# Row slots of the expert routing worked out tile by tile between later score maxima, and fewer zero products on TensorE

## The chip, the cores and the metric

The kernel runs on one core of a Trainium2 chip. The metric is the device time of one execution in microseconds (us). The engines are TensorE (PE, with its weight loads as PEld), VectorE (DVE), ScalarE (ACT), GpSimd (POOL) and SyncE (SP), which here only issues DMAs. Each runs its own list of instructions in order and waits on semaphores for the others.

## The reference

For x of 1024 tokens by 256 columns, xn is x normalised per row, and the result is x + attention(xn) + experts(xn).

```python
q, k, v = xn @ wq.T, xn @ wk.T, xn @ wv.T          # 16 heads of 16, q and k rotated (RoPE)
scores = where(causal, -inf, q @ k.T / sqrt(16))
att = softmax(scores) @ v @ wo.T
logits = xn @ gate_weight.T                         # 64 experts, 8 for each token
topk_w, topk_idx = top_k(softmax(logits), 8); topk_w /= sum(topk_w)
# each token's row goes to its 8 experts, rows of one expert stand together
out = (silu(rows @ w_gate[e]) * (rows @ w_up[e])) @ w_down[e]
y = sum(out of the token's 8 rows * topk_w)
```

## The kernel before, in words

The front part normalises x, projects it, rotates q and k, splits them in a high and a low part and stores these parts in DRAM (`qk_parts`). The 16 heads are worked in 4 groups of 4 (`g` from 0 to 3). For each group SP loads the parts back in the layout that the scores want (`stage(g, c)`, once for each half `c` of the 1024 tokens), into `qz` and `kz`. `stage(0, 1)`, the second half of group 0, is issued when the last store of `qk_parts` has landed.

The softmax needs the largest score of each query ahead of the scores themselves. So each group has two passes. The first pass is made of 38 "max" units: PE computes a block of up to 512 score columns into one of three PSUM banks (`max_scores`, L1001 and the mask L1005), and DVE reduces it (`use_max`, L1449). A bank is free when DVE has reduced the unit three places ahead. When the first half's maxima are there (`neg`, c = 0, behind the third block of query tile 7), PE transposes them (L1019), DVE negates them into `neg_hi` and `neg_lo` (L1462, L1463), and SP writes them as two more rows of `qz` (`place_negmax`, L495). The second pass then computes the scores (`scores`, L1030, L1033), ACT takes the exponentials (L825), and PE multiplies them with v (`pv`, L1047). Its 12 steps go through key tiles; steps 0 to 3 belong to the first half of the queries, steps 4 to 11 to the second half, and step 4 waits for the second `neg`.

The order in which max units stand between score steps is written out by `attention_order` from the table `MAXIMA_AT`, whose entries say how many 128-column blocks are to be done by which step. `g = -1` is the stretch ahead of the first score. In it and in steps 0 to 3 of group 0 (`FILL_UNTIL = CT`, CT is 4) each max unit is followed by one product of zeros into an unused bank (`keep_busy`, L1011).

The experts' routing lies beside this. PE counts the choices (`counts`, banks 3 and 4), DVE makes from the counts the first row of each expert and a map of row numbers (`count_and_map`, L1336 to L1339), and for each of the 8 token tiles three small instructions: eight row numbers per token, the same beside the token's row, and the same as integers (L1343, L1344, L1346). In the kernel before all of that stands on DVE ahead of the first maximum. POOL waits for each tile's numbers and sends the tile's rows to DRAM with 8 indirect DMAs (L733, 64 in all). SP waits for all 64 and loads the experts' rows (`load_rows`, L525, L527). The experts run between group 1 and group 2 and begin on PE with L1088.

Of the kernel before, what the change touches and what calls it, by code (L numbers as in the profile page):

```python
# [10 lines left out]
ALU = mybir.AluOpType  # L11
# [6 lines left out]
NT = N // P  # L18
# [8 lines left out]
K = 8  # L27
# [8 lines left out]
ID, SLOT_AT = D, D + K  # L36
# [5 lines left out]
SLOT_BASE = float(1 << 14)  # L42
# [7 lines left out]
B_BANKS, PV_BANK, A_BANKS = (0, 1, 2), 3, (5, 6, 7)  # L50
RING, GU_BANKS, EXTRA_BANK = (0, 1, 2), (5, 3), 7
HALF = N // 2
CT = NT // 2
SLOTS = 3
STEPS = [(0, kt) for kt in reversed(range(CT))] + [(1, kt) for kt in reversed(range(NT))]
NS = len(STEPS)
MAXIMA_AT = ((-1, NS, 68), (0, CT, 176), (0, NS, 296), (1, NS, 504), (2, NS, 576))
SUMS_FROM = 20
FILL_UNTIL = CT
EXIT_FILL = 4  # L60
TABLES_AT, RANKS_AT = 4, 7
OUT_START, LAST_OUT = 14, 36
# [13 lines left out]
def queries(step):  # L76

    half, kt = STEPS[step]
    return max(kt * P, half * HALF), (half + 1) * HALF


def attention_order():
# [19 lines left out]
    for g in range(-1, G + 1):  # L102
        for step in range(NS):
            for j in range(HG):
# [5 lines left out]
                if g == G - 1:  # L110
                    for c, start, count in ((0, OUT_START, NT), (1, LAST_OUT, CT)):
                        n = step * HG + j - start
                        here += [("att", c, n)] if 0 <= n < count else []
                        here += [("out", c, n - 1)] if 1 <= n <= count else []
                marks = [((m, e), units) for m, e, units in MAXIMA_AT]
                now = (g, step + 1)
                share = MAXIMA_AT[-1][2]
                for (at_0, units_0), (at_1, units_1) in zip([((-1, 0), 0)] + marks, marks):
# [26 lines left out]
def build(nc, x, cos, sin, w_in, w_out, w_gu, w_down, out):  # L145
    ctx = ExitStack()
    with ctx:
        def sb(name, shape, dt=F32):
            return ctx.enter_context(nc.sbuf_tensor(name, shape, dt))

        def sem(name):
            return ctx.enter_context(nc.semaphore(name))
# [14 lines left out]
        rows = rows_sb[:, 0:NT * XR].rearrange("p (t d) -> p t d", d=XR)  # L167
# [28 lines left out]
        logits, slot_map = (routing[:, a, :].rearrange("p (t e) -> p t e", e=E) for a in range(2))  # L196
# [4 lines left out]
        slot_f = sb("slot_f", [P, NT, K])  # L201
        slot_i = sb("slot_i", [P, NT, K], I32)
# [143 lines left out]
        s_smap = sem("counts_used")  # L346
        s_slotf = sem("slots_found")
        s_sloti = sem("slot_numbers")
        s_pad = sem("row_ends_set")
        s_w = sem("rank_weights")  # L350
        s_row = sem("row_slots_set")
# [51 lines left out]
        a_no = {unit: n for n, unit in enumerate(a_order)}  # L403
# [10 lines left out]
        def b_no(g, step, j):  # L414

            return (g * NS + step) * HG + j
# [44 lines left out]
        def _(sp):  # L461
# [52 lines left out]
            def registers(table, top):  # L514

                _, v = nc.values_load_multi_w_load_instructions(
                    table, engines=[mybir.EngineType.SP], min_val=0, max_val=top,
                    skip_runtime_bounds_check_because=BOUNDED)
                return v
# [399 lines left out]
        def _(pe):  # L919
# [89 lines left out]
            def keep_busy(bank, times=1):  # L1009
                for _ in range(times):  # L1010
                    pe.matmul(ps[:, bank, :], zero_b[:, :], fill_b[:, :], start=True, stop=True)  # L1011
# [25 lines left out]
            def pv(g, step):  # L1037

                half, kt = STEPS[step]
                lo, hi = queries(step)  # L1040
                pe.wait_ge(s_be, b_no(g, step, HG - 1) + 1)
                if step in (0, CT):
                    if g >= 1:
                        pe.wait_ge(s_acc, 2 * (g - 1) + half + 1)
                    pe.matmul(ps[:, PV_BANK + half, :], zero_b[:, :], fill_b[:, :], start=True, stop=True)
                for j in range(HG):
                    last = pe.matmul(ps[VW * j:VW * j + VC, PV_BANK + half, lo % HALF:HALF],  # L1047
                                     v_aug[:, kt, g * HG + j, :], probs[:, step % 2, j, lo % HALF:HALF],
                                     start=False, stop=True, skip_group_check=True)
                last.then_inc(s_pv, 1)  # L1050
# [126 lines left out]
            def experts():  # L1177
                pe.wait_ge(s_ad, a_before)
                transpose_pair(0, 0)
                transpose_pair(0, 1)  # L1180
                transpose_spare(0)
                pe.wait_ge(s_acc, 2 * BEFORE_EXPERTS)
                for n in range(NG):
                    gate_up(n, 0)
                    if n == NG - 1:
                        spill_transpose(0)
                    gate_up(n, 1)
                    if n == NG - 1:
                        spill_gate_up(0)
                        more = load_more(pe)  # L1190
                    if n + 1 < NG:
                        transpose_pair(n + 1, 0)
                        transpose_spare(n + 1)
                    pe.wait_ge(s_wd[n % 2], 16 * (n // 2 + 1))
                    down(n, 0)
                    if n + 1 < NG:
                        transpose_pair(n + 1, 1)
                    down(n, 1)
                    spare_down(n)
                    if 0 <= n - TABLES_AT < 2:  # L1200
                        spread_columns(n - TABLES_AT)
                keep_busy(GU_BANKS[0], 2)
                spill_down(0)
                keep_busy(GU_BANKS[0], EXIT_FILL)
                loop_groups(pe, more, spill_group)
                pe.wait_ge(s_ye, 2 * NG)
                pe.wait_ge(s_sye, more * TURN + 1)
# [3 lines left out]
            for g in range(-1, G + 1):  # L1211
                if g == BEFORE_EXPERTS:
                    pv(g - 1, NS - 1)
                    experts()
                for step in range(NS):
                    half, kt = STEPS[step]
                    if step in (0, CT) and 0 <= g < G:
                        pe.wait_ge(s_negd[g % SLOTS][half], 32 * (g // SLOTS + 1))
                    if step == 0 and g == 0:
                        pe.wait_ge(s_smap, 1)  # L1220
                    for j in range(HG):
                        if 0 <= g < G:
                            scores(g, step, j)
                        for kind, *what in a_at[(g, step, j)]:
                            make[kind](*what)
                            if kind == "max" and (g, step) < (0, FILL_UNTIL):
                                keep_busy(PV_BANK + 1 if g == 0 else B_BANKS[0])
                        if j == 1 and 0 <= g < G and step >= 1:
                            pv(g, step - 1)
                        if j == 1 and g >= 1 and g != BEFORE_EXPERTS and step == 0:  # L1230
                            pv(g - 1, NS - 1)
# [14 lines left out]
        def _(dve):  # L1246
            chained = [0]

            def link(ins):
                chained[0] += 1  # L1250
                ins.then_inc(s_vchain, 1)
                dve.wait_ge(s_vchain, chained[0])
# [74 lines left out]
            def by_expert(vector):  # L1327
                return vector[:, :].rearrange("p (a e) -> p a e", a=1).to_broadcast([P, NT, E])

            dve.wait_ge(s_const, CONSTS)  # L1330

            def count_and_map():
                dve.wait_ge(s_cnt, 1)
                dve.wait_ge(s_ones, 1)
                counted = ps[:, 4, :].rearrange("p (t e) -> p t e", e=E)
                link(dve.tensor_copy(cnt[:, :], ps[:, 3, 0:E]))  # L1336
                link(dve.tensor_tensor_scan(c_end[:, :], ones[:, 0:E], cnt[:, :], 0.0, ALU.mult, ALU.add))
                link(dve.scalar_tensor_tensor(first_row[:, :], c_end[:, :], 1.0, cnt[:, :], ALU.add, ALU.subtract))
                link(dve.tensor_tensor(slot_map[:, :, :], counted, by_expert(first_row), ALU.add))  # L1339
                dve.sem_inc(s_smap, 1)  # L1340
                dve.wait_ge(s_pad, 1)
                for t in range(NT):
                    dve.max(slot_f[:, t, :], slot_map[:, t, :]).then_inc(s_slotf, 1)  # L1343
                    dve.max(rows[:, t, SLOT_AT:SLOT_AT + K], slot_map[:, t, :]).then_inc(s_row, 1)  # L1344
                    dve.wait_ge(s_slotf, t + 1)
                    dve.tensor_scalar(slot_i[:, t, :], slot_f[:, t, :], -1.0 - SLOT_BASE, None, ALU.add).then_inc(s_sloti, 1)  # L1346

            count_and_map()

            def differences():  # L1350
                dve.tensor_tensor(logits[:, :, :], logits[:, :, :], top_v[:, :, 0:1].to_broadcast([P, NT, E]),
# [276 lines left out]
            for g in range(-1, G + 1):  # L1628
                if g == BEFORE_EXPERTS:
                    experts()  # L1630
                for step in range(NS):
                    for j in range(HG):
                        for kind, *what in a_at[(g, step, j)]:
                            use[kind](*what)
                        turn = ((g - BEFORE_EXPERTS) * NS + step) * HG + j - SUMS_FROM
                        if 0 <= turn < NT * K:
                            sum_rank(turn // K, turn % K)
                    if (g, step) in prepare:
                        prepare[(g, step)]()
# [38 lines left out]
```

## Time and profile before

| | |
|---|---|
| median of 3 runs | 383.92 us (383.39 to 386.04) |
| the profiled execution | 381.56 us, of which its span in the trace is 379.8 us |
| stretch ahead of the first score | ends at 60.1 us of the span |
| group 0, steps 0 to 3 | 60.1 to 81.99 us |
| group 0, steps 4 to 11, and group 1 | to 158.4 us |
| experts | to about 295 us |

Times in the rows below are us from the start of the span, unless marked ns. In a timeline row the first number is the start, the second how long it took, and a bracket at the end says how long the engine was idle before it and what ended that. `x4` is a count of merged instructions.

### The profile page before, as it was taken

How to read it: one execution, taken by the hardware profiler on the slowest of the kernel's cores; microseconds unless marked ns; L12 is line 12 of the kernel's file. 1: busy time of each engine (PE TensorE's matmuls, PEld its weight loads, DVE VectorE, ACT ScalarE, POOL GpSimd, SP SyncE). 2: the span in 40 equal slices, each digit the busy share in tenths (PEclk: the TensorE clock that was granted, in tenths of full speed). 3: DMA queues.
4: the chain of work that ended last, by engine and by line, in shares of the span. 5: the costliest groups of instructions: out<-in, count | busy, mean ns of one | idle time of the engine just before them, and what ended most of it. 6: DMA issues, size and time to landing. Idle time of an engine off the chain costs nothing.

```text
span 379.8 us, 7229 instructions
## 1 busy us (share of the span) xinstructions
PE 346.9 (91%) x2264; PEld 231.1 (61%) x2264; DVE 266.4 (70%) x654; ACT 170.3 (45%) x373; POOL 169.4 (45%) x195
## 2 busy tenths in 40 slices
PE   1999499999999999899999999999999999699883
PEld 1465254554456555488888888888896554345432
DVE  5798878778877778745577766677763389868822
ACT  6243661326545554433343333344332667263751
POOL 5655877777777100016665566665664400000000
PEclk9999879999999999999999999999999999889999
DMA  7036876869438663038999898989972480190011
GB/s 254 17 114 197 262 225 183 263 175 301 160 115 209 181 184 117 4 121 251 339 349 304 266 323 288 314 269 325 316 233 70 131 357 3 25 418 3 2 57 55
DMA packets 38903, 73.87 MB, mean 194 GB/s; under 512 B 7094, under 2 KB 25801, under 8 KB 37840
## 3 DMA queue, kind: packets, MB, share of 16 engines
q1 hardware_dynamic: 31344, 55.67, 46.8%
q0 software_dynamic: 6960, 17.32, 13.1%
q8 instruction: 19, 0.31, 0.4%
q10 hardware_dynamic: 560, 0.41, 0.3%
q14 instruction: 20, 0.16, 0.1%
HBM read 50.41 MB, written 25.05 MB: 199 GB/s over the span
## 4 chain that ended last, share of the span: by engine, by line
PE 73%; DVE 16%; DMA 3%; issue 3%; POOL 1%; ACT 1%; SPq 1%; DVEq 0%; ACTq 0%; POOLq 0%
PE ps L1114 19%; PE ps L1001 10%; PE ps L1030 8%; PE ps L1123 7%; PE ps L1047 7%; DVE x_sb L1617 6%; PE ps L1088 4%; PE ps L1011 3%; PE ps L1130 2%; PE ps L933 2%; PE ps L1005 2%; DVE mx_low L1449 2%; DVE mx L1449 2%; PE ps L1033 2%; DMA x_sb<-x 1%
## 5 line engine op out<-in xcount | busy, mean ns | idle before, releaser
L825 ACT ACTIVATE probs<-ps 128x512 f32<-128x512 f32 (+3 forms) x192 | 88.2, 491 | 90.5 <-PE ps L1033 59.4
L738 POOL DMA_INDIRECT rank_results<-work,dst x81 | 80.2, 990 | 93.7 <-DVE dst L1537 69.8
L1001 PE MATMUL ps<-kz,qz 96*128 96x512 f32 (+3 forms) x192 | 75.6, 433 | 5.1 <-DVE mx L1449 3.6
L1030 PE MATMUL ps<-qz,kz 128*128 128x512 f32 (+3 forms) x192 | 76.7, 428 | 2.4 <-issue 1.1
L733 POOL DMA_INDIRECT expert_rows<-rows,slot_i x64 | 61.7, 964 | 20.2 <-issue 19.2
L1449 DVE TENSOR_REDUCE mx<-ps 128x1 f32<-128x512 f32 (+3 forms) x88 | 53.7, 639 | 14.4 <-PE ps L1005 12.3
L1030 PEld LDWEIGHTS ps<-qz,kz 128*128 128x128 f32 x192 | 37.8, 199 | 35.7 <-ACT probs L825 19.9
L1449 DVE TENSOR_REDUCE mx_low<-ps 128x1 f32<-128x512 f32 x64 | 41.7, 685 | 18.1 <-PE ps L1001 16.4
L1001 PEld LDWEIGHTS ps<-kz,qz 96*128 96x128 f32 x192 | 38.5, 202 | 11.4 <-DVE mx L1449 5.1
L1047 PE MATMUL ps<-probs,v_aug 128*20 128x512 f32 (+3 forms) x384 | 41.5, 505 | 1.9 <-ACT probs L825 1.9
L837 ACT ACTIVATE work<-ps 96x320 f32<-96x320 f32 x32 | 13.9, 433 | 61.3 <-PE ps L1114 61.3
L1505 DVE SCALAR_TENSOR_TENSOR work<-work,ps 96x320 f32<-96x320 f32 x32 | 15.5, 483 | 36.0 <-ACT work L837 33.5
L1114 PE MATMUL ps<-work,gate_up_first 128*96 128x160 f32 x256 | 36.6, 301 | 1.1 <-DVE work L1522 1.1
L1114 PEld LDWEIGHTS ps<-work,gate_up_first 128*96 128x96 f32 x256 | 34.6, 163 | 3.9 <-issue 3.8
L1114 PE MATMUL ps<-work,gate_up_second 128*96 128x160 f32 x256 | 36.8, 301 | 0.0
L1114 PEld LDWEIGHTS ps<-work,gate_up_second 128*96 128x96 f32 x256 | 34.6, 163 | 3.4 <-issue 3.4
L1617 DVE SCALAR_TENSOR_TENSOR x_sb<-work,w_rank,x_sb 128x256 f32<-128x256 f32 x64 | 30.8, 482 | 6.2 <-DMA work<-rank_results 3.3
L1033 PE MATMUL ps<-mask_kq,ident_b 128*128 128x128 bf16 x128 | 30.0, 236 | 0.0
L1005 PE MATMUL ps<-ident_b,mask_kq 128*128 128x128 bf16 x128 | 29.2, 237 | 0.0
L857 ACT ACTIVATE work<-ps 128x256 f32<-128x256 f32 x64 | 21.1, 381 | 17.9 <-PE ps L1123 17.9
L1005 PEld LDWEIGHTS ps<-ident_b,mask_kq 128*128 128x128 bf16 x128 | 12.8, 100 | 14.5 <-issue 9.9
L1011 PE MATMUL ps<-fill_b,zero_b 128*128 128x512 bf16 x53 | 21.2, 412 | 0.0
(184 smaller groups left out, 460.2 us busy)
## 6 DMA issues: line engine op xcount, KB each, us to landing
rows<-expert_rows SPq DMA_DIRECT2D x64, 136.0 KB
work<-rank_results SPq DMA_DIRECT2D x8, 1024.0 KB, 8.8
gate_up_first<-w_gu SPq DMA_DIRECT2D x8, 768.0 KB, 5.8
gate_up_second<-w_gu SPq DMA_DIRECT2D x8, 768.0 KB
qz<-qk_parts SPq DMA_DIRECT2D x16, 256.0 KB, 6.0
rows<-w_down SPq DMA_DIRECT2D x8, 384.0 KB, 4.6
down_second<-w_down SPq DMA_DIRECT2D x8, 384.0 KB
rows<-expert_rows SPq DMA_DIRECT2D x68, 34.0 KB
```

The lines of the kernel that those rows point to most:

```text
L733: pool.indirect_dma_start(xd[:, :], bass.IndirectOffsetOnAxis(ap=slot_i[:, t, k:k + 1], axis=0), rows[:, t, :], None).then_inc(s_scat, 16)
L738: pool.indirect_dma_start(yd[:, :], bass.IndirectOffsetOnAxis(ap=at, axis=0), source, None, bounds_check=N * K - 1, oob_is_err=False).then ...
L825: act.activation(probs[:, step % 2, j, lo % HALF:HALF], ps[:, B_BANKS[n % len(B_BANKS)], lo % HALF:HALF], ACT.Exp, scale=DK ** -0.5).then_ ...
L1001: last = pe.matmul(bank[:, n * width:(n + 1) * width], head_rows(qz, g, j, i, 96), kz[g % SLOTS][0:96, lo // HALF, j, 0:width], start=True ...
L1005: last = pe.matmul(bank[:, (n + 1) * width - P:(n + 1) * width], mask_kq[:, :], ident_b[:, :], start=False, stop=True, skip_group_check=True)
L1011: pe.matmul(ps[:, bank, :], zero_b[:, :], fill_b[:, :], start=True, stop=True)
L1030: last = pe.matmul(bank[:, a:HALF], head_rows(kz, g, j, kt, P), qz[g % SLOTS][:, half, j, a:HALF], start=True, stop=True, skip_group_check ...
L1033: last = pe.matmul(bank[:, a:a + P], ident_b[:, :], mask_kq[:, :], start=False, stop=True, skip_group_check=True)
L1047: last = pe.matmul(ps[VW * j:VW * j + VC, PV_BANK + half, lo % HALF:HALF], v_aug[:, kt, g * HG + j, :], probs[:, step % 2, j, lo % HALF:HALF],
L1114: last = pe.matmul(bank[:, w * CAP:(w + 1) * CAP], wgu[b][:, at:at + I], xT[b][:, 2 * p + e, c, :], start=(c == 0), stop=(c == DC - 1))
L1449: dve.tensor_reduce(best, bank, AX.X, ALU.max).then_inc(s_ad, 1)
L1617: last = dve.scalar_tensor_tensor(x_sb[:, t, :], gathered[t % GBUFS][:, k, :], w_rank[:, t, k:k + 1], x_sb[:, t, :], ALU.mult, ALU.add)
```

## The change

Three things change. First, `count_and_map` and the eight slot computations no longer stand on DVE ahead of all maxima. `count_and_map` and the slots of tile 0 stand behind the first `neg` (group 0, first half); the slots of tile 1 to 7 stand behind the seven units that follow, one tile behind each. Second, `MAXIMA_AT` puts 52 instead of 68 blocks ahead of the first score, which is 14 max units instead of 18, the last of them the unit right ahead of the first `neg`; the units between `neg` and the first score move in between the scores of steps 0 to 3. Third, the zero products follow the 14 max units ahead of the first score only; the 33 behind later units are gone. The wait for the counts' banks moves from the first score to the first `pv`.

```diff
-MAXIMA_AT = ((-1, NS, 68), (0, CT, 176), (0, NS, 296), (1, NS, 504), (2, NS, 576))
+MAXIMA_AT = ((-1, NS, 52), (0, CT, 176), (0, NS, 296), (1, NS, 504), (2, NS, 576))
 SUMS_FROM = 20
-FILL_UNTIL = CT
...
                 pe.wait_ge(s_be, b_no(g, step, HG - 1) + 1)
+                if (g, step) == (0, 0):
+                    pe.wait_ge(s_smap, 1)
...
-                    if step == 0 and g == 0:
-                        pe.wait_ge(s_smap, 1)
...
                             make[kind](*what)
-                            if kind == "max" and (g, step) < (0, FILL_UNTIL):
-                                keep_busy(PV_BANK + 1 if g == 0 else B_BANKS[0])
+                            if kind == "max" and g < 0:
+                                keep_busy(B_BANKS[0])
...
                 dve.sem_inc(s_smap, 1)
                 dve.wait_ge(s_pad, 1)
-                for t in range(NT):
-                    dve.max(slot_f[:, t, :], slot_map[:, t, :]).then_inc(s_slotf, 1)
-                    dve.max(rows[:, t, SLOT_AT:SLOT_AT + K], slot_map[:, t, :]).then_inc(s_row, 1)
-                    dve.wait_ge(s_slotf, t + 1)
-                    dve.tensor_scalar(slot_i[:, t, :], slot_f[:, t, :], -1.0 - SLOT_BASE, None, ALU.add).then_inc(s_sloti, 1)
-
-            count_and_map()
+
+            def slots(t):
+
+                dve.max(slot_f[:, t, :], slot_map[:, t, :]).then_inc(s_slotf, 1)
+                dve.max(rows[:, t, SLOT_AT:SLOT_AT + K], slot_map[:, t, :]).then_inc(s_row, 1)
+                dve.wait_ge(s_slotf, t + 1)
+                dve.tensor_scalar(slot_i[:, t, :], slot_f[:, t, :], -1.0 - SLOT_BASE, None, ALU.add).then_inc(s_sloti, 1)
...
                             use[kind](*what)
+                            turn = a_no[(kind, *what)] - a_no[("neg", 0, 0)]
+                            if turn == 0:
+                                count_and_map()
+                            if 0 <= turn < NT:
+                                slots(turn)
```

On DVE, before, from the last low part of the front on (`routing` is the row map and `rows` the token rows):

```order
L1287 TENSOR_TENSOR part_lo<-ps,part_hi 128x4x128
L1336 COPY cnt<-ps 128x64
L1337 SCALAR_TENSOR_TENSOR c_end<-ones,cnt 128x64
L1338 SCALAR_TENSOR_TENSOR first_row<-c_end,cnt 128x64
L1339 TENSOR_TENSOR routing<-ps,first_row 128x512
L1343 MAX slot_f<-routing 128x8
L1344 MAX rows<-routing 128x8
L1346 TENSOR_SCALAR slot_i<-slot_f 128x8
```

On DVE with the change, from the first maximum on:

```order
L1449 TENSOR_REDUCE mx<-ps 128x1 x8
L1449 TENSOR_REDUCE mx<-ps 128x2 x2
L1449 TENSOR_REDUCE mx<-ps 128x4
L1449 TENSOR_REDUCE mx_low<-ps 128x1 x3
L1462 TENSOR_SCALAR neg_hi<-ps 16x128
L1463 SCALAR_TENSOR_TENSOR neg_lo<-ps,neg_hi 16x128
L1336 COPY cnt<-ps 128x64
...
L1348 TENSOR_SCALAR slot_i<-slot_f 128x8
L1449 TENSOR_REDUCE mx_low<-ps 128x1
L1345 MAX slot_f<-routing 128x8
L1346 MAX rows<-routing 128x8
L1348 TENSOR_SCALAR slot_i<-slot_f 128x8
```

The counts and the slots have moved from ahead of the first maximum to behind the first `neg`, and from the second tile on a maximum stands between two tiles' slots.

On PE, before, around the first `neg` (L1019) and the first score (L1030):

```order
L1019 MATMUL ps<-ident,mx 16x128
L1001 MATMUL ps<-kz,qz 128x512
L1011 MATMUL ps<-fill_b,zero_b 128x512
L1001 MATMUL ps<-kz,qz 128x512
L1005 MATMUL ps<-ident_b,mask_kq 128x128
L1011 MATMUL ps<-fill_b,zero_b 128x512
L1001 MATMUL ps<-kz,qz 128x512
L1005 MATMUL ps<-ident_b,mask_kq 128x128
L1011 MATMUL ps<-fill_b,zero_b 128x512
L1001 MATMUL ps<-kz,qz 128x512
L1005 MATMUL ps<-ident_b,mask_kq 128x128
L1011 MATMUL ps<-fill_b,zero_b 128x512
```

On PE with the change, at the same place (the line numbers are one lower):

```order
L1018 MATMUL ps<-ident,mx 16x128
L1029 MATMUL ps<-qz,kz 128x128
L1032 MATMUL ps<-mask_kq,ident_b 128x128
L1000 MATMUL ps<-kz,qz 128x512 x2
L1004 MATMUL ps<-ident_b,mask_kq 128x128
L1029 MATMUL ps<-qz,kz 128x128
L1032 MATMUL ps<-mask_kq,ident_b 128x128
L1000 MATMUL ps<-kz,qz 128x512
L1004 MATMUL ps<-ident_b,mask_kq 128x128
```

The four max units that stood between `neg` and the first score now stand behind it, two to a score, and no zero product stands between them.

## Rows read from the trace of the kernel before

**Rows 1.** The page: the span.
```profile
span 379.8 us, 7229 instructions
```
**Rows 2.** Busy time in stretches, count in brackets; after POOL: granted clock, DMA share, GB/s.
```profile
core 0: us, PE busy (x) PEld busy (x) DVE busy (x) ACT busy (x) POOL busy (x), PEclk, DMA share, GB/s
43.30:46.50 3.20, 0.00 (x0) 0.00 (x1) 3.15 (x24) 1.16 (x2) 1.89 (x3) 0.86 0.58 208
46.50:52.40 5.90, 5.90 (x21) 3.44 (x21) 4.17 (x8) 5.90 (x4) 4.38 (x6) 0.50 0.77 203
60.10:81.99 21.89, 21.89 (x145) 12.13 (x146) 17.52 (x32) 6.99 (x16) 16.71 (x18) 1.00 0.74 214
60.89:78.42 17.53, 17.53 (x119) 9.54 (x118) 14.83 (x26) 5.52 (x13) 13.32 (x14) 1.00 0.79 234
95.30:158.41 63.11, 61.80 (x401) 33.76 (x401) 50.59 (x93) 32.70 (x66) 23.02 (x24) 1.00 0.48 144
315.00:318.00 3.00, 3.00 (x24) 1.57 (x20) 2.95 (x6) 2.17 (x4) 0.00 (x0) 1.00 0.00 0
```
**Rows 3.** Timeline of PE, 41 to 82 us.
```profile
41.39 0.50 PE L1001 MATMUL ps<-kz,qz 96*128 96x512 f32 x1 [0.40 <-DVE part_lo L1287]
46.50 0.79 PE L1001 MATMUL ps<-kz,qz 96*128 96x512 f32 x1 [3.29 <-DVE mx L1449]
49.05 0.88 PE L1001 MATMUL ps<-kz,qz 96*128 96x384 f32 x1
49.92 0.88 PE L1001 MATMUL ps<-kz,qz 96*128 96x384 f32 x1
54.61 0.47 PE L1001 MATMUL ps<-kz,qz 96*128 96x512 f32 x1 [0.48 <-issue]
81.99 0.41 PE L1030 MATMUL ps<-qz,kz 128*128 128x128 f32 x1
```
**Rows 4.** Source line of the query loads, issued around 48 us: stage(0, 1).
```profile
L488 SPq DMA_DIRECT2D qz<-qk_parts x2: 432/508/584, 48.0 to 48.6; - x2
DMA to landing us min/median/max: 5.3/5.6/5.9
```
**Rows 5.** The same line, issued around 35 us: stage(0, 0).
```profile
L488 SPq DMA_DIRECT2D qz<-qk_parts x2: 432/508/584, 34.7 to 35.3; - x2
DMA to landing us min/median/max: 4.2/4.5/4.7
```
**Rows 6.** Timeline of DVE, 41 to 79 us.
```profile
41.25 0.22 DVE L1336 COPY cnt<-ps 128x64 f32<-128x64 f32 x1
43.26 0.22 DVE L1343 MAX8 slot_f<-routing 128x8 f32<-128x64 f32 x1
45.76 3.14 DVE L1449 TENSOR_REDUCE mx<-ps 128x1 f32<-128x512 f32 x5
60.89 0.69 DVE L1449 TENSOR_REDUCE mx<-ps 128x1 f32<-128x512 f32 x1 [0.76 <-PE ps L1005]
78.11 0.28 DVE L1463 SCALAR_TENSOR_TENSOR neg_lo<-ps,neg_hi 16x128 fp32r<-16x128 f32 x1
```
**Rows 7.** The chain of waits, 38 to 62 us: start, us of the chain, what.
```profile
55.12 1.89 DVE mx_low L1449 x3
57.22 0.29 DVE neg_lo L1463
58.16 1.89 DMA qz<-neg_lo
60.85 0.21 PE ps L1011
```
**Rows 8.** Source line of the row scatters on POOL: ns min/median/max, first and last start.
```profile
L733 POOL DMA_INDIRECT expert_rows<-rows,slot_i x64: 956/960/1192, 44.5 to 124.4; - x64
```
**Rows 9.** Timelines of SP and PE where the experts begin.
```profile
131.17 1.99 SPq L525 DMA_DIRECT2D rows<-expert_rows x4
159.40 1.09 PE L1088 MATMUL ps<-ident,rows 128*128 128x128 f32 x8
```

## Prediction

> **What bounds the kernel now.** I read the stretches first, then the two timelines around the first score, then the loads that both wait for. From the first score on PE sets the pace: it is busy 21.89 of 21.89 us in steps 0 to 3 of group 0, and 61.80 of 63.11 us from 95.3 us to the experts [rows 2]. A delay or a gain of PE at step 4 therefore reaches the end nearly one for one. Ahead of the first score PE isn't the bound. It begins the maxima at 41.39 us, fills its three banks and then waits 3.29 us for DVE [rows 3], which first makes the counts and all eight slots, from 41.25 to 45.76 us [rows 6]. In that pause the granted clock falls: 0.86 on average over the wait, 0.50 (the 1.2 GHz level) from 46.5 to 52.4 us [rows 2]. That looks like the loss, and the change is aimed at it. But the end of the stretch is set elsewhere. The twelfth unit is the first that reads the second half of the tokens, and it starts at 54.61 us after 0.48 us of idle that nothing in the row explains [rows 3]. The second query load of that half was issued at 48.6 us and took up to 5.9 us [rows 4]: it landed at 54.5. So what DVE did early, it did in time that the load left over anyway. From there 2.9 us lead to the end of `neg_lo` at 57.51, and the placement by DMA to the first score at 60.1 [rows 7].
>
> **Up to the first score.** (1) The load. The same load of the first half took at most 4.7 us [rows 5]; the scatters, the first of them at 44.5 us [rows 8], were not yet running then. With the change they start near 60 us, so I take 1.2 us off: landing at 53.3. Bounds: 54.5 (nothing gained) and 52.1 (twice as much).
>
> (2) The eleven units before that. DVE starts them near 42 instead of 45.76, and needs about 0.6 us for each (3.14 us for five [rows 6]), so it is through at about 48.5. Then PE has nothing to do until 53.3. That is longer than the 3.29 us after which the clock stood at half, so PE restarts at half: the first unit takes 0.79 us, and a unit with its zero product 0.88 (two starts 0.87 apart) [rows 3]. Unit fourteen is done at 53.4 + 0.79 + 2 x 0.88 = 55.95. A zero product and the transposition take some 0.95 (an estimate, twice what they take before), and the two negations 0.6: `neg_lo` ends at 57.5. Before it ended at 57.51. The early landing and the low clock cancel. At full clock it would be 53.4 + 2.9 = 56.3, which is 1.2 better. I keep 57.5, and with the same placement the first score at 60.1.
>
> (3) Counts and slots of tile 0. They now stand behind `neg_lo`, in the 2.6 us in which PE and DVE wait for the placement (57.51 to 60.1 [rows 7]). Before, they took 2.0 us up to the second slot's start [rows 6]. They are hidden; without that cover they would cost those 2.0.
>
> **From the first score to step 4.** (4) PE. Of its 21.89 us, 29 zero products of 0.21 [rows 7] go, which is 6.1; the four units that moved in add about 1.2 (0.3 each, an estimate: 0.88 at half clock is 0.44 at full, less 0.21, plus the wider block). That leaves 17.0, and step 4 at 77.1 instead of 81.99. If PE alone counted, this would be a gain of 4.9 us.
>
> (5) DVE. It is busy 14.83 of the 17.53 us between its first reduction there and the second `neg` [rows 2]. The change adds four units at 0.61 (14.1 us without the `neg` pair and the small maximum, over 23 units) and seven slots at 0.36 (43.26 to 45.76 for seven [rows 6]), together 2.4 + 2.5. That makes 19.75 us of work in a stretch that lasted 17.53. DVE is then the bound and has no idle time left: from 60.9 [rows 6] to 80.65. Step 4 waits for the second placement, 2.6 us as for the first, so its first score comes at 83.3 instead of 81.99: +1.3 us. Bounds: a slot between two reductions may cost 0.7, double, which adds another 2.4; below the back-to-back price it can't go on an engine that takes its list in order.
>
> (6) The clock in that stretch. PE comes to the first score after another pause, at half clock. At half its 33 units cost 2 x 17.0 / 33 = 1.03 us each, with their share of scores and `pv`. While DVE does slots (seven pairs of 0.61 + 0.36, until 67.6 us) that is about DVE's own pace. After that DVE needs 0.61, and each us at half clock loses 0.41. Before, the full clock came back 5.9 us after dense work began at 46.5 [rows 2]. From 60.1 that gives 66.0 and a price of 0; counted from 67.6, since PE isn't dense before, it gives 73.5 and a price of 2.4. I take 70 us and 1.0.
>
> (7) What hangs on the slots. POOL takes the 64 scatters at its own pace, 44.5 to 124.4 us [rows 8]. They begin some 16 us later and end so. Behind the wait for them SP holds the row loads, the weights of the first two rounds and the placements of groups 2 and 3; the row loads go at 147 instead of 131.17 [rows 9]. PE wants the rows at 159.40 [rows 9], now near 162. Eight issues at 0.5 and a landing of 6 make 10 us, so 4 to 5 remain: cost nothing, and one for one beyond that. The wait for the counts at the first `pv` is met by then.
>
> The sum is 0 + 1.3 + 1.0 = +2.3 us. On the profiled execution (381.56, span 379.8 [rows 1]) that is 383.9. That execution lies 2.36 below the median of the runs shown, 383.92, so the forecast in the median's terms is 386.2. A measurement of this kernel can tell about 1%, 3.84 us, from no change.
>
> **Rivals.** (A) Half clock stays, slower. Place: steps 0 to 3 of group 0. With no zero products PE pauses at each unit for a bank. The price beyond 1.3 is 0.41 for each us past 67.6, and it decides from a return later than 73.8 us. At 76 us it is 3.4, so +4.7: 388.6. In the extreme PE stays at half to step 4: 34 us from 60.1, +12, 396. For it: the clock fell in the one pause shown [rows 2]. Against it: PE at half has more to do than DVE after 67.6, so it has no pauses left; and from 315 to 318 us, where DVE is busy 2.95 of 3.00 us, the clock stays at 1.00 [rows 2]. The Trainium skill, "TensorE: Matmul & The Clock Gate", section "A second HAM failure mode: psum-queue depth-cycling", tells of a kernel that went through its PSUM banks with small idle times between groups of matmuls, in which the clock swung between its two levels. By that page the extreme, 396, would be the time; the row at 315 us doesn't agree with it.
>
> (B) The load lands at 52.1 and the clock is full from then on: `neg_lo` at 55.1, 2.4 earlier; with +1.3 that is -1.1, 382.8. For it: the DMA engines were 0.77 busy from 46.5 to 52.4 us [rows 2], so scatters and loads were in each other's way. Against it: the long pause of PE.
>
> (C) PE, not DVE, paces steps 0 to 3, and the removed products come out in full: -4.9, 379.0. Against it: the sum in (5), which has only trace durations in it.
>
> (D) The scatters' delay reaches the experts. With 5 us of cover gone and 5 more, 391.
>
> **Chances.** Forecast 0.53, A 0.24 (of it 0.04 for the extreme), B 0.15, C 0.04, D 0.04. The range from 382.4 (B with half a us of spread) to 389.4 (A with a little more than its price) leaves out C, D and the extreme of A. Faster by over 1% is C and a rest of B, 0.06. Slower by over 1% is A, D and the upper edge of the forecast (two-fold slots), 0.29. Within 1%: 0.65.
>
> **What would show it.** Right: a pause of PE of 5 us ahead of its twelfth unit, which starts near 53.4; granted clock 0.50 behind it; first score near 60; no zero products behind it and PE waiting for DVE's reductions up to 82; DVE without idle time from 61 to 80; step 4 near 84; last scatter near 140. Wrong: a first score before 58 (then the load gained more than thought), PE dense between 60 and 77 (then the bound in (5) is wrong), the clock at half past 74 us (A), or PE waiting for rows at 160 (D).

## The result, and the profile after

The changed kernel takes 393.11 us (median of 4 runs, 392.45 to 404.4) against 384.5 us of the kernel before in the same runs: 2.2% slower, ratio 1.0216 with a 95% interval of 1.0167 to 1.0266. The forecast was 386.2, the range ended at 389.4. Here and in the ratios below, a run that took over 1.5% longer than the fastest of its kernel does not count (here the one at 404.4 us). The profiled execution took 393.27 us, its span is 391.5.

The page of the changed kernel: the granted clock in 40 slices of 9.8 us (tenths of full speed).

```profile
span 391.5 us, 7164 instructions
...
PEclk9999955559999999999999999999999999899998
```

The kernel before had its half clock in one short piece (46.5 to 52.4 us, [rows 2]). Here slices 6 to 9 stand at 5: the trace has the clock at half (0.50 granted, the 1.2 GHz level) from 50.1 to 87.6 us. Busy time in stretches of the changed kernel (columns as in [rows 2]):

```profile
48.00:54.30 6.30, 0.15 (x1) 0.00 (x0) 0.66 (x1) 6.03 (x4) 0.00 (x0) 0.67 0.72 161
54.30:60.70 6.40, 3.19 (x7) 1.17 (x7) 4.47 (x12) 0.00 (x0) 0.00 (x0) 0.50 0.01 4
60.73:66.00 5.27, 5.27 (x19) 3.55 (x19) 4.09 (x17) 0.90 (x4) 3.63 (x4) 0.50 0.95 215
66.00:69.50 3.50, 3.39 (x10) 1.97 (x9) 3.50 (x14) 0.98 (x3) 2.59 (x4) 0.50 1.05 270
69.50:72.90 3.40, 3.40 (x19) 1.73 (x19) 1.71 (x4) 0.60 (x2) 2.66 (x3) 0.50 1.03 312
...
76.30:79.70 3.40, 3.40 (x19) 1.88 (x17) 1.34 (x3) 0.49 (x1) 2.49 (x4) 0.50 0.25 91
...
84.20:87.60 3.40, 3.40 (x17) 1.40 (x16) 2.90 (x7) 0.60 (x1) 2.52 (x3) 0.50 0.32 122
60.73:87.60 26.87, 26.75 (x105) 15.85 (x105) 19.62 (x51) 5.81 (x14) 20.05 (x21) 0.50 0.63 182
87.70:91.10 3.40, 3.35 (x22) 2.03 (x19) 2.32 (x6) 1.20 (x2) 2.48 (x4) 1.00 0.57 118
```

Three things are to be seen. PE is all but idle from 48 to 54.3 us, and half idle to 60.7. From the first score on it is busy nearly without a break, and from 69.5 us on DVE is not (1.71 of 3.40, 1.34 of 3.40): there PE at half clock, not DVE, paces the stretch. And being busy did not bring the clock back soon: PE is busy 26.75 of the 26.87 us from the first score to 87.6 us, at 0.50.

The timeline of PE, to be read against [rows 3] (first maximum, the unit behind the load, first score, first score of step 4):

```profile
41.49 0.47 PE L1000 MATMUL ps<-kz,qz 96*128 96x512 f32 x1 [0.50 <-DVE part_lo L1286]
...
54.33 0.77 PE L1000 MATMUL ps<-kz,qz 96*128 96x512 f32 x1 [6.18 <-issue]
...
60.73 0.47 PE L1029 MATMUL ps<-qz,kz 128*128 128x128 f32 x1 [3.21 <-DMA qz<-neg_lo]
...
91.13 0.31 PE L1029 MATMUL ps<-qz,kz 128*128 128x128 f32 x1
```

Before, the unit behind the load started at 54.61, the first score at 60.1, step 4 at 81.99. So the pause of 3.29 us ahead of the fourth unit is gone, the pause ahead of the load has grown from 0.48 to 6.18, the first score is 0.6 us later, and step 4 is 9.1 us later: 30.4 us from the first score to step 4 instead of 21.9. That is the loss. From step 4 to the end of the span the profiled runs differ by another 2.6 us (300.4 against 297.8). They arise in the last group of heads (54.3 us from its first score to the end of the span, against 51.8), where the half-clock pieces lie otherwise (three of 3.4 us against one of 6.8). The profiled runs of the kernels below take 297.4 to 301.2 us from step 4 to the end, but for c_front with 308.2, whose half clock reaches past step 4. I count the 2.6 us as spread of the runs, but that is not shown: the profiles with a zero product behind every early unit lie at 297.4 to 299.3 us, those without any in steps 0 to 3 at 298.9 to 300.7, c_front apart, with one profile of each kernel.

DVE and the scatters did what was forecast. Timeline of DVE (last early maximum, end of the placement, counts, first slot, last slot):

```profile
47.97 0.69 DVE L1449 TENSOR_REDUCE mx<-ps 128x4 f32<-128x512 f32 x1 [0.22 <-PE ps L1004]
...
57.87 0.28 DVE L1463 SCALAR_TENSOR_TENSOR neg_lo<-ps,neg_hi 16x128 fp32r<-16x128 f32 x1
...
58.36 0.23 DVE L1336 COPY cnt<-ps 128x64 f32<-128x64 f32 x1 [0.21 <-DVE neg_lo L1463]
...
60.31 0.16 DVE L1348 TENSOR_SCALAR slot_i<-slot_f 128x8 int32<-128x8 f32 x1
...
67.44 0.24 DVE L1348 TENSOR_SCALAR slot_i<-slot_f 128x8 int32<-128x8 f32 x1
```

The source line of the scatters on POOL (count, shortest, median and longest in ns, first to last in us, what it waited for):

```profile
L732 POOL DMA_INDIRECT expert_rows<-rows,slot_i x64: 957/963/1192, 61.5 to 141.5; - x64
```

The eleven early units are through at 48.7 us, the counts and the first slot fit between `neg_lo` and the first score, the last slot is there at 67.7 us. SP's row loads went at 145.05 us and PE took the rows at 168.45, with nothing to wait for.

### The profile page after: what moved, and what is told of

The parts are those of the page before. It is cut to its first block, busy times and chain, and to the rows that moved or that the text cites. A ratio compares the mean times of both kernels' runs of the same rounds, so it can differ in the third digit from the quotient of the medians.

```text
span 391.5 us, 7164 instructions
## 1 busy us (share of the span) xinstructions
PE 353.0 (90%) x2231; PEld 236.2 (60%) x2231; DVE 266.2 (68%) x654; ACT 170.2 (43%) x373; POOL 169.6 (43%) x195
## 4 chain that ended last, share of the span: by engine, by line
PE 72%; DVE 16%; issue 5%; DMA 3%; POOL 1%; SPq 1%; ACT 1%; DVEq 0%; ACTq 0%; POOLq 0%
PE ps L1115 18%; PE ps L1000 10%; PE ps L1029 8%; PE ps L1124 7%; PE ps L1048 7%; DVE x_sb L1617 6%; PE ps L1089 4%; PE ps L1131 2%; DVE mx L1449 2%; DVE mx_low L1449 2%; PE ps L1004 2%; PE ps L932 2%; PE ps L1078 2%; PE ps L1032 2%; DMA x_sb<-x 1%
## 5 line engine op out<-in xcount | busy, mean ns | idle before, releaser
L1000 PE MATMUL ps<-kz,qz 96*128 96x512 f32 (+3 forms) x192 | 78.8, 456 | 7.7 <-issue 6.2
L732 POOL DMA_INDIRECT expert_rows<-rows,slot_i x64 | 61.8, 965 | 37.2 <-issue 19.2
L1449 DVE TENSOR_REDUCE mx<-ps 128x1 f32<-128x512 f32 (+3 forms) x88 | 53.3, 638 | 17.0 <-PE ps L1004 15.6
L1029 PEld LDWEIGHTS ps<-qz,kz 128*128 128x128 f32 x192 | 39.1, 207 | 39.8 <-ACT probs L824 19.3
L1000 PEld LDWEIGHTS ps<-kz,qz 96*128 96x128 f32 x192 | 41.7, 222 | 13.8 <-issue 6.9
L1048 PE MATMUL ps<-probs,v_aug 128*20 128x512 f32 (+3 forms) x384 | 42.4, 515 | 1.6 <-ACT probs L824 1.6
L836 ACT ACTIVATE work<-ps 96x320 f32<-96x320 f32 x32 | 13.9, 434 | 61.2 <-PE ps L1115 61.2
L1617 DVE SCALAR_TENSOR_TENSOR x_sb<-work,w_rank,x_sb 128x256 f32<-128x256 f32 x64 | 30.8, 482 | 6.7 <-DMA work<-rank_results 3.8
L1032 PE MATMUL ps<-mask_kq,ident_b 128*128 128x128 bf16 x128 | 31.0, 244 | 0.0
L1004 PE MATMUL ps<-ident_b,mask_kq 128*128 128x128 bf16 x128 | 30.5, 246 | 0.0
L1032 PEld LDWEIGHTS ps<-mask_kq,ident_b 128*128 128x128 bf16 x128 | 13.2, 103 | 14.3 <-issue 9.4
## 6 DMA issues: line engine op xcount, KB each, us to landing
rows<-w_down SPq DMA_DIRECT2D x8, 384.0 KB
down_second<-w_down SPq DMA_DIRECT2D x8, 384.0 KB
```

What stands on the lines that cost most here:

```text
L732: pool.indirect_dma_start(xd[:, :], bass.IndirectOffsetOnAxis(ap=slot_i[:, t, k:k + 1], axis=0), rows[:, t, :], None).then_inc(s_scat, 16)
L1000: last = pe.matmul(bank[:, n * width:(n + 1) * width], head_rows(qz, g, j, i, 96), kz[g % SLOTS][0:96, lo // HALF, j, 0:width], start=True ...
L1004: last = pe.matmul(bank[:, (n + 1) * width - P:(n + 1) * width], mask_kq[:, :], ident_b[:, :], start=False, stop=True, skip_group_check=True)
L1029: last = pe.matmul(bank[:, a:HALF], head_rows(kz, g, j, kt, P), qz[g % SLOTS][:, half, j, a:HALF], start=True, stop=True, skip_group_check ...
L1032: last = pe.matmul(bank[:, a:a + P], ident_b[:, :], mask_kq[:, :], start=False, stop=True, skip_group_check=True)
L1449: dve.tensor_reduce(best, bank, AX.X, ALU.max).then_inc(s_ad, 1)
```

## The experiments

Theory 1 is that the clock falls in the pauses ahead of the first score and comes back quickly only where zero products stand behind it. Theory 2 is that the clock is a bystander and the slots between maxima, or the later scatters, are the cost. Times from the first score to step 4 are read from each profiled run's timeline; they are 21.9 us before and 30.4 us with the change.

| kernel | ratio to before (95%) | first score | step 4 | between them | half clock before step 4 |
|---|---|---|---|---|---|
| before | 1 | 60.1 | 82.0 | 21.9 | 45.6 to 52.4 |
| the change | 1.0216 (1.0167 to 1.0266) | 60.7 | 91.1 | 30.4 | 50.1 to 87.6 |
| a_fill | 1.0109 (1.0072 to 1.0146) | 61.6 | 88.5 | 27.0 | 51.2 to 68.3 |
| b_nofill | 0.9954 (0.9912 to 0.9996) | 61.3 | 80.4 | 19.1 | 46.3 to 53.2 |
| c_front | 1.0219 (1.0151 to 1.0288) | 61.8 | 93.6 | 31.8 | 46.5 to 53.3, 60.2 to 114.8 |
| d_bridge | 1.0223 (1.0154 to 1.0293) | 60.7 | 91.5 | 30.8 | 62.4 to 89.7 |
| e_bridge_full | 1.0179 (1.0100 to 1.0258) | 60.1 | 87.5 | 27.4 | 66.7 to 76.9 |
| f_bridge_and_fill | 1.0062 (1.0029 to 1.0096) | 61.3 | 87.0 | 25.7 | none |
| g_slots_alone | 1.0107 (1.0072 to 1.0142) | 62.2 | 86.7 | 24.5 | 51.0 to 61.2 |
| h_52_alone | 1.0134 (1.0058 to 1.0211) | 61.6 | 88.4 | 26.7 | 44.3 to 51.1, 57.9 to 68.2 |
| i_fill_two_steps | 0.9957 (0.9928 to 0.9987) | 62.1 | 82.3 | 20.2 | short pieces to 59.0 |
| j_fill_every_second | 0.9965 (0.9927 to 1.0002) | 61.8 | 81.9 | 20.2 | 48.1 to 51.5 |
| k_nofill_no_pause | 0.9934 (0.9904 to 0.9965) | 62.7 | 81.9 | 19.1 | 43.2 to 50.0, 56.8 to 60.2 |

The first maximum itself starts between 41.4 and 43.2 us in these runs, up to 1.8 us apart, so the time between first score and step 4 is the column to compare.

**a_fill.** The changed kernel with the zero products put back; the wait for the counts' banks goes back to the first score with them (not in the cut below).

```diff
-                            if kind == "max" and g < 0:
-                                keep_busy(B_BANKS[0])
+                            if kind == "max" and (g, step) < (0, CT):
+                                keep_busy(PV_BANK + 1 if g == 0 else B_BANKS[0])
```

> The changed kernel with the zero products put back behind each max unit of steps 0 to 3. Theory 1 (the clock falls in the 6 us pause ahead of the load and comes back only where zero products stand): full clock some 6 to 10 us after the first score at 60.7, step 4 near 87 instead of 91.1, about 389 us. Theory 2 (the clock is not the cost; slots between maxima or the later scatters are): the 29 and more products of 0.2 to 0.4 us come on top, step 4 at 97 or later, 399 us.

It took 387.81 us. Stretches of a_fill:

```profile
61.50:64.90 3.40, 3.33 (x12) 2.00 (x13) 2.04 (x8) 0.56 (x2) 2.15 (x2) 0.50 0.93 222
64.90:68.30 3.40, 3.40 (x14) 1.85 (x11) 3.06 (x12) 0.28 (x1) 2.63 (x3) 0.51 1.05 236
68.30:88.50 20.20, 20.20 (x134) 10.89 (x134) 17.44 (x38) 6.17 (x13) 15.32 (x17) 1.00 0.56 165
```

The clock is back 6.7 us after the first score, where the change without zero products needed 26.9. PE has 33 products more to do and takes 3.4 us less from the first score to step 4 (27.0 against 30.4). Theory 2, which has the products come on top (399 us), falls as the whole account.

**b_nofill.** The kernel before with the zero products of steps 0 to 3 left out, nothing else.

```diff
-FILL_UNTIL = CT
+FILL_UNTIL = 0
```

> The kernel before, with the zero products of steps 0 to 3 left out and all else as it was; PE comes to the first score at full clock. Theory 1a (a clock that is full stays full without them): DVE and PE pace the stretch at about 18 us, step 4 near 79, 381 us, faster than before by 3. Theory 1b (zero products are needed to hold the clock too): it falls soon after 60 us, step 4 near 90, 393 us. Theory 2 (the clock is not the cost): as 1a.

It took 383.03 us against 384.0. Its stretch from the first score to step 4:

```profile
61.30:80.40 19.10, 18.20 (x117) 11.02 (x117) 16.86 (x33) 6.99 (x16) 14.53 (x16) 1.00 0.81 218
```

Full clock throughout, 2.8 us shorter than before: theory 1a for this run. The third part of the change is by itself a small gain. But three of its ten runs took 386.6 to 389.8 us at a mean clock of 0.946 to 0.959, against 0.972 to 0.982 in the others; with them the median is only 0.25% better, and where the clock was lost in those is not known, since only the first run was profiled.

**c_front.** The changed kernel with counts and slots back ahead of the first maximum; 52 blocks, no zero products behind the first score.

```diff
+            count_and_map()
+            for t in range(NT):
+                slots(t)
...
-                            if turn == 0:
-                                count_and_map()
-                            if 0 <= turn < NT:
-                                slots(turn)
```

> The changed kernel with counts and slots back ahead of the first maximum; 14 units ahead of the first score and no zero products behind it. Theory 1: the clock has come back by 52.4 as before; whether the 3 us pause for the placement takes it again decides: 381 us if not, 391 or more if so, and the granted clock says which. Theory 2 (slots between maxima are the cost): 383 us whatever the clock.

It took 392.99 us. PE waited 4.0 us for the placement ahead of the first score, the clock fell at 60.2 us, and without zero products it stayed down. The profiled run (403.5 us) is the longest of the four, so its row in the table, and the 114.8 us above all, stand for that run alone. The others were at 390.4 to 395.1 us with a mean clock of 0.939 to 0.943 (0.911 in the profiled run), about as low as the change's 0.938 to 0.939. So the whole loss is there without a slot between maxima, as theory 1 had it for a clock taken by that pause (391 or more); theory 2 said 383.

**d_bridge and e_bridge_full.** The changed kernel with zero products in its two pauses, 26 and 10 in the first of these kernels, 30 and 17 in the second.

```diff
-                                keep_busy(B_BANKS[0])
+                                keep_busy(B_BANKS[0], LOAD_FILL if what == [0, 0, 0] else 1)
+                            if kind == "neg" and what == [0, 0]:
+                                keep_busy(B_BANKS[0], NEG_FILL)
```

> The changed kernel with 26 zero products in the pause ahead of the load and 10 in the pause for the placement. Theory 1: no half clock before the first score; step 4 near 83 as the DVE sum has it, 385 us. If a full clock has to be held by zero products, it falls in steps 0 to 3 all the same, and the time is 391. Theory 2: no gain over the changed kernel, 393 us.

> The changed kernel with 30 zero products ahead of the load and 17 ahead of the placement, so that PE has no pause before the first score; none behind it. In the run with 26 and 10 a pause of 1.6 us was left and the clock fell 1.7 us after the first score. If the pause did that: full clock through steps 0 to 3 as in the run without zero products on the old order, step 4 near 83, 385 us. If PE paced by DVE's slots can't hold the clock without zero products: it falls between 62 and 69 us all the same, 391 us.

They took 391.63 and 389.97 us. In d_bridge PE came to the first score at full clock after a remaining pause of 1.6 us, and the clock fell at 62.4. In e_bridge_full PE had no pause there (0.06 us), and the clock fell at 66.7. Stretches of e_bridge_full with three units of PE in the second of them, and below it two of b_nofill, which held the clock:

```profile
59.90:63.30 3.40, 2.96 (x16) 1.74 (x15) 2.47 (x9) 0.83 (x3) 2.15 (x2) 1.00 0.91 211
63.30:66.70 3.40, 2.19 (x9) 1.27 (x9) 3.40 (x17) 0.66 (x2) 2.49 (x3) 1.00 1.07 239
66.70:70.10 3.40, 3.14 (x17) 1.33 (x15) 3.01 (x8) 0.38 (x1) 2.49 (x4) 0.50 1.04 271
66.70:76.94 10.24, 9.98 (x45) 5.31 (x43) 7.47 (x15) 2.13 (x5) 7.80 (x9) 0.50 0.73 219
...
63.53 0.47 PE L1001 MATMUL ps<-kz,qz 96*128 96x512 f32 x1 [0.44 <-DVE mx L1452]
64.45 0.51 PE L1001 MATMUL ps<-kz,qz 96*128 96x512 f32 x1 [0.31 <-DVE mx L1452]
65.38 0.50 PE L1001 MATMUL ps<-kz,qz 96*128 96x512 f32 x1 [0.43 <-DVE mx L1452]
```

```profile
60.00:63.41 3.41, 2.43 (x14) 1.36 (x13) 2.66 (x6) 0.55 (x2) 2.50 (x4) 1.00 0.75 191
63.30:66.70 3.40, 3.24 (x20) 2.04 (x18) 3.40 (x8) 1.06 (x4) 2.76 (x3) 1.00 0.96 236
```

From 63.3 to 66.7 us DVE is busy all the time in both. In e_bridge_full it does slots between its reductions, each unit of PE waits for a reduction, PE gets 9 matmuls into 3.4 us (2.19 busy), and the clock falls; in b_nofill it does reductions alone, PE gets 20 (3.24 busy) and keeps it. So bridging the pauses is not enough. That the slots took the clock, by thinning PE out, is the likely reading and more than theory 1 said, but it is not shown: the two kernels differ in the blocks ahead of the first score too, a bridged kernel without slots between maxima was not run, and b_nofill also held its clock through a stretch with PE busy 2.43 of 3.41 us. In both bridged kernels the second of their expectations is what came (about 391 us). In e_bridge_full the clock was back after 10.2 us, with no zero product behind a unit; in d_bridge it took 27.3 us.

**f_bridge_and_fill.** e_bridge_full with the zero products of a_fill too.

> As the last one, and zero products behind each max unit of steps 0 to 3 too. Both forms of the clock theory: full clock from 41 us to step 4; then the time is DVE's sum of the prediction, step 4 near 83.3 (+1.3), 385.3 us. If slots between maxima cost more than 0.36 us each, or the later scatters slow something, step 4 is later at full clock.

It took 386.68 us, ratio 1.0062: the clock never falls before step 4, and the loss shrinks from 2.2% to 0.6%. Its stretch:

```profile
61.27:86.97 25.70, 25.08 (x156) 13.48 (x157) 22.23 (x56) 7.00 (x16) 19.20 (x20) 1.00 0.69 185
```

So by the ratios the clock was some two thirds and more of the loss. But 25.7 us at full clock is not the 23.2 that my DVE sum gave (60.1 to 83.3); PE is busy 25.08 of them. Four more units with their products than before (0.5 each, an estimate from 0.3 and 0.21) are 2 of the 3.8 us that the stretch is longer than before; the rest is open.

**g_slots_alone and h_52_alone.** The first part of the change alone, and the second alone, each with the zero products.

```diff
 g: a_fill with
-MAXIMA_AT = ((-1, NS, 52), ...
+MAXIMA_AT = ((-1, NS, 68), ...
 h: the kernel before with
-MAXIMA_AT = ((-1, NS, 68), ...
+MAXIMA_AT = ((-1, NS, 52), ...
```

> The kernel before with counts and slots moved as in the change, and nothing else: 68 blocks ahead of the first score, zero products behind every max unit to step 3. Clock theory: half from about 50 us, full again 6 to 10 us after PE restarts at 54.3, since zero products stand there; step 4 near 85, 387 us. Rival (the moved slots are the cost, not the products left out): the whole 8 to 9 us stand here, 392 us.

> The kernel before with 52 instead of 68 blocks ahead of the first score, and nothing else; counts and slots first, zero products to step 3. Clock theory: a pause of 3 us for the placement, perhaps half clock behind it for 3 to 7 us, PE paces steps 0 to 3 with 4 units more; step 4 at 84 to 86, 386 to 388 us. If the order of units costs nothing: 384 us.

They took 387.48 and 389.06 us. In g the pause ahead of the load (6.5 us) takes the clock and zero products have brought it back at 61.2, a little before the first score. With full clock the stretch is 24.5 us instead of 21.9, and the first score is later: moving DVE's slots behind the load costs by itself some 1.1%, the half clock ahead of the first score included. The rival's 392 us did not come. In h the clock falls at 57.9, only 0.2 us into the pause for the placement (3.9 us); in the 3.4 us before that PE was busy 1.74, and its pause of 2.3 us ahead of the load reaches into them. With zero products it is back at 68.2. The median lies 1 us above the range expected.

```profile
54.53:57.94 3.41, 1.74 (x7) 0.71 (x7) 1.45 (x3) 1.05 (x1) 2.50 (x4) 1.00 0.58 192
57.90:61.60 3.70, 0.00 (x0) 0.00 (x0) 0.94 (x3) 0.00 (x0) 2.79 (x4) 0.51 0.35 120
61.60:68.20 6.60, 6.56 (x23) 3.69 (x23) 3.46 (x5) 0.83 (x3) 5.08 (x6) 0.50 0.91 225
68.20:88.40 20.20, 20.20 (x137) 11.02 (x136) 16.94 (x30) 6.17 (x13) 15.32 (x17) 1.00 0.58 184
```

**i, j and k.** Since b_nofill had gained, three kernels look for what of the zero products can go on the old order: products in steps 0 and 1 only (`FILL_UNTIL = 2`), behind every second unit, and none in steps 0 to 3 with four more ahead of the first score, where PE paused 0.9 us:

```diff
 k: the kernel before with FILL_UNTIL = 0 and
-                                keep_busy(PV_BANK + 1 if g == 0 else B_BANKS[0])
+                                keep_busy(B_BANKS[0], 5 if what == [0, 7, 6] else 1)
```

> The kernel before, with zero products behind the max units of steps 0 and 1 only (none in steps 2 and 3). Clock theory: in steps 2 and 3 PE is dense by itself, so the clock stays full in every run; some 18 products of 0.21 us less, step 4 some 2 us earlier (the stretch of 21.9 us becomes 20), 382 us against 384, and no run with a long half clock. If PE loses the clock there too, single runs near 388.

> The kernel before, with a zero product behind every second max unit of steps 0 to 3. Clock theory: half as many hold the clock; 15 products less, stretch of 20 us or DVE's pace, 382 us. Rival (DVE paces the stretch once some products are gone): no more than 1 us off, 383.

> The kernel before without zero products in steps 0 to 3, and with four more behind the last unit ahead of the first score, which fill PE's pause of 0.9 us there. Without these four 3 of 10 runs were at 387 to 390 with a lower mean clock. If that pause decides it: all runs near 381 to 383. If the DVE-paced step 0 decides it: still some runs near 389.

They took 382.35, 385.1 and 382.12 us against 384.17. The stretches are 20.2, 20.2 and 19.1 us at full clock from 60.2 us on at the latest. i came as expected. k has the lowest ratio: 0.7% below the kernel before (interval 0.4 to 1.0%), its longest of twelve runs at 385.11 us, where b_nofill had reached 389.8. The differences between k, i and b_nofill are within their intervals. j had four of twelve runs at 386.5 to 387.4, which its expectation did not foresee, and by the median of all twelve it gained nothing; its profiled run lost time near the end (301.2 us from step 4), not in this stretch: it has a half clock from 297.3 to 304.1 us that the profile of the kernel before has not. Why is open.

## Why the prediction was wrong

The direction was right, the size was not: +2.3 us forecast, +8.6 in the medians. The step that failed is (6), the price of the clock in steps 0 to 3. I put the return of the full clock at 70 us and 1.0 us on it. It came at 87.6, and a_fill, which differs by the zero products (and where the counts are waited for, a wait over by then), shows why: with them 68.3, without them 87.6. The argument that misled is in rival A, "PE at half has more to do than DVE after 67.6, so it has no pauses left". PE had next to no pauses even before that, 0.12 us from the first score on, against the "PE isn't dense before" of (6), and the clock stayed at half for 26.9 us all the same. The return 5.9 us after dense work in [rows 2], which I took as the pattern, was that of dense work with zero products between the units; I treated those products as cost alone. Rival A had the place, 0.24 of the chance and, with a return at 88 us, nearly the size: 0.41 x (87.6 - 67.6) is 8.2, with the 1.3 of (5) 9.5, against 9.1 at step 4. Its cause, that PE pauses at each unit for a bank, is not what the trace shows. The page of the Trainium skill that stood with it ("TensorE: Matmul & The Clock Gate", section "A second HAM failure mode: psum-queue depth-cycling") tells of a clock that swings between its levels when PE idles briefly between groups of matmuls; the extreme that I took from it does not follow from a swing. Here PE hardly idled, and the clock did not swing but stayed low, and came back before step 4.

The other steps, in their order:

- (1) The load was to land at 53.3. PE took it at 54.33, 0.3 us sooner than before, not 1.2. The gain was a quarter of what the first half's latency [rows 4, 5] had suggested. The load was also issued 0.3 us later than before (48.9 instead of 48.6). That the scatters slow it is not shown: its longest landing is 5.3 us in g, where none runs beside it, and 5.4 in h, 5.9 before and 6.2 in c_front, where they do. Mis-sized.
- (2) The eleven units were through at 48.7 (48.5 forecast), and PE restarted at half clock, as said. `neg_lo` ended at 58.15 instead of 57.5: the unit behind the load started 0.9 us later than the 53.4 of the sum, and the rest took 0.3 less. The first score came at 60.7.
- (3) Counts and slot 0 between `neg_lo` and the first score: right.
- (4) The removed products as a gain of PE: right where the clock holds. b_nofill shows 2.8 us of the 6.1; DVE (16.86 of 19.10 us busy) is near its own limit there, but PE is still busy 18.20, and why it needs so long is not shown.
- (5) DVE paces the slots' part: DVE is busy throughout from 62.5 to 69.5 us (3.50 of 3.50 in the last of it), but so is PE at half clock (3.39 of 3.50), so which of them paces can't be read off there, and behind it PE was slower. No run bears out its size of 1.3 us: the slots alone, with zero products, cost 2.6 us in the stretch and 1.1% in all (g), and with full clock the changed order with products took 25.7 us (f). The changed order without products never ran at full clock throughout, so what (5) costs by itself stays open.
- (7) Scatters and row loads: right, covered, with loads at 145 us for a forecast of 147.

How the parts work together: the removal of the products alone gains 0.5%; 52 blocks alone lose 1.3%; slots alone lose 1.1%. 52 blocks and slots with products (a_fill) lose 1.1%, and 52 blocks without products and without moved slots (c_front) lose 2.2%, as much as the whole change. Behind a pause the products brought the clock back in 6.5 to 6.7 us (h, a_fill), where the changed kernel needed 26.9. The change made the pauses longer and took this repair away.

## What to carry to other kernels

Ask of work that seems useless on PE what clock it holds or brings back, and price a removal together with the pauses that stand ahead of it: here leaving out 29 products gained 0.5% on the old order, and leaving out 33 lost 1.1% on the new one. A wait that ends at the same late transfer whatever is done before it is free time; here moving seven slots of 0.36 us out of it, into a stretch where DVE was nearly full, cost 2.6 us there (g). And busy time of PE is not evidence for its clock: read the granted clock beside it.

## What the runs showed of the hardware that was not expected

PE busy 26.75 of 26.87 us at the lower level did not bring the upper one back before 87.6 us, in float32 products of 128 to 512 columns, masks and `pv`. With one 512-column bfloat16 product of zeros for each max unit it came back 6.5 to 6.7 us after the first score (h_52_alone, a_fill). Without them the time at the lower level differed widely: 10.2 us in e_bridge_full, 27.3 in d_bridge, and to 114.8 us in the one long run of c_front. A full clock held without the products where PE was busy 3.24 and 2.43 of 3.4 us (b_nofill), and fell where PE was busy 2.19 of 3.40 between DVE's slots (e_bridge_full). What about these products the clock answers to was not tried.
